# Attention layer of a four-layer graph network: the weighting of the values moves from ScalarE and GpSimd to VectorE

## What is computed

```
q_dst, k_src, v_src = Q[dst], K[src], V[src]
score = sum(q_dst * k_src, axis=-1) / sqrt(16)
attn  = softmax(clip(score, -5, 5), axis=0)     # over all edges, per head
h_out = zeros_like(Q).at[dst].add(attn[..., None] * v_src)
```

## Time and profile before

| | |
|---|---|
| median of 3 runs | 6164.49 us (6153.3 to 6164.83) |
| profiled execution | 6162.2 us, of which the span is 6160.4 us |
| TensorE busy over the span | 5555.2 us (90%) |
| VectorE busy | 4416.3 us (72%) |
| ScalarE busy | 2019.9 us (33%) |
| GpSimd busy | 1360.3 us (22%) |
| the attention's edge stage | from 1076 to 3257 us of the span |
| in it: TensorE / VectorE / ScalarE / GpSimd | 2057.67 / 1666.68 / 868.58 / 724.43 us |

### The profile page before, as it was taken

One profiled execution on the slowest core, in us unless ns is written; L12 is line 12 of the kernel. 1 busy time (PEld: TensorE's weight loads), 2 busy tenths in 40 slices (PEclk: granted clock), 3 DMA queues, 4 the chain that ended last, 5 costly groups with the idle time before them and its releaser, 6 DMA issues. The chain is left out here.

```text
span 6160.4 us, 165256 instructions
## 1 busy us (share of the span) xinstructions
PE 5555.2 (90%) x58225; PEld 4851.5 (79%) x58310; DVE 4416.3 (72%) x7547; ACT 2019.9 (33%) x4615; POOL 1360.3 (22%) x1304
## 2 busy tenths in 40 slices
PE   3999988999999999999996879999999998699986
PEld 2888876888888888888885569999999996456655
DVE  7999942777777777777774457777777774388874
ACT  0000033333433434433432322222222221266651
POOL 1444445333333333333332310000000000200000
PEclk9999999999999999999998989999999997899988
DMA  6444412222222222222220123333333330100000
GB/s 122 149 158 149 158 56 79 88 88 85 85 85 85 88 86 82 88 88 81 88 80 18 37 98 117 121 118 118 115 123 117 119 115 34 57 5 0 0 1 22
DMA packets 206210, 523.66 MB, mean 85 GB/s; under 512 B 33555, under 2 KB 85398, under 8 KB 199318
## 3 DMA queue, kind: packets, MB, share of 16 engines
q1 hardware_dynamic: 195936, 518.35, 24.7%
q10 hardware_dynamic: 10179, 4.02, 0.3%
HBM read 485.12 MB, written 37.19 MB: 85 GB/s over the span
## 5 line engine op out<-in xcount | busy, mean ns | idle before, releaser
L1279 PE MATMUL ps<-kv_table,stage 128*128 128x256 bf16 x7644 | 1252.5, 273 | 29.4 <-DVE stage L1135 27.3
L1251 POOL TENSOR_TENSOR message<-message 128x512 f32<-128x512 f32 (+1 forms) x676 | 724.4, 1072 | 1468.9 <-ACT message L1213 1468.9
L1294 PE MATMUL ps<-message,slot_hot 128*128 128x136 f32 x5200 | 779.2, 292 | 121.2 <-POOL message L1251 102.6
L1667 PE MATMUL ps<-a_table,stage 128*128 128x128 bf16 x7644 | 843.7, 219 | 31.3 <-DVE stage L1550 31.3
L1670 PE MATMUL ps<-window,stage 128*128 128x128 bf16 x7800 | 861.3, 219 | 0.0
L1282 PE MATMUL ps<-window,stage 128*128 128x128 bf16 x7800 | 860.6, 219 | 0.0
L1294 PEld LDWEIGHTS ps<-message,slot_hot 128*128 128x128 f32 x5200 | 649.2, 190 | 212.1 <-POOL message L1251 167.8
L1142 DVE TENSOR_TENSOR slot_hot<-iota,slots 128x512 f32<-128x512 f32 (+1 forms) x676 | 452.5, 669 | 452.7 <-PE ps L1294 452.7
L1569 DVE TENSOR_TENSOR slot_hot<-iota,slots 128x512 f32<-128x512 f32 (+1 forms) x676 | 454.1, 672 | 416.5 <-PE ps L1682 401.4
L1620 ACT ACTIVATE edge<-ps 128x512 f32<-128x512 f32 x624 | 373.4, 598 | 1105.9 <-PE ps L1682 1068.8
L1279 PEld LDWEIGHTS ps<-kv_table,stage 128*128 128x128 bf16 x7644 | 669.1, 98 | 71.5 <-issue 27.9
(11 more groups left out here) (335 smaller groups left out, 7606.3 us busy)
## 6 DMA issues: line engine op xcount, KB each, us to landing
stage<-lists SPq DMA_DIRECT2D x312, 768.0 KB, 4.1
edges<-in_edge_attr SPq DMA_DIRECT2D x52, 1984.0 KB, 7.6
stage<-lists SPq DMA_DIRECT2D x104, 896.0 KB, 5.4
window<-qkv_rows SPq DMA_DIRECT2D x52, 288.0 KB, 4.7
qkv_rows<-kv_table SPq DMA_DIRECT2D x26, 384.0 KB, 2.5
window<-ab_rows SPq DMA_DIRECT2D x52, 192.0 KB, 4.3
qkv_rows<-q_parts SPq DMA_DIRECT2D x26, 192.0 KB, 2.0
ab_rows<-a_table SPq DMA_DIRECT2D x26, 192.0 KB, 2.0
```

What stands on the lines that cost most here:

```text
L1251: pool.tensor_tensor(values, values, message[n % 2][:, 0:nt, D:D + HEADS].unsqueeze(3) .broadcast_to([P, nt, HEADS, HEAD]), ALU.mult).then ...
L1279: nc.tensor.matmul(kv_ps[n % 2][:, i, :], from_src, kv_table[:, tile, q, :], start=(q == 0), stop=(q == 2))
L1294: last = nc.tensor.matmul(ps[:, 6 + d, 0:D + HEADS], slot_hot[n % 2][:, i, :], message[n % 2][:, i, :], start=(tile == 0), stop=(tile == S ...
L1667: nc.tensor.matmul(edge_ps[n % 2][:, i, :], from_src, a_table[:, tile, q, :], start=(q == 0), stop=False)
```

## The change

ScalarE no longer copies V, and GpSimd has no program in this stage. A new VectorE instruction multiplies V, still in PSUM, by the weights and writes `message`. On VectorE `slot_hot` moves from the head of the batch to behind `clipped`, with the new instruction behind it. On ScalarE `exp(n)` now comes ahead of `keep(n+1)`, and it is `exp` that waits for the scatter that frees `message`. A gather waits for `q_kept1` (Q copied) and `message1` (V multiplied) of the batch that used its PSUM buffers.

```diff
                     def batch(pair, g, n):
                         b, s = n % BATCHES, pair * NB2 + n
                         nt = len(batch_tiles(b))
-                        dve.wait_ge(scattered1, s + 1)
-                        dve.tensor_tensor(slot_hot[n % 2][:, 0:nt, :], over_chunks(iota1[:, :], nt),
...
-                        dve.wait_ge(v_kept1, s + 3)
+                        dve.wait_ge(q_kept1, s + 3)
                         dve.wait_ge(score1, s + 1)
...
                         dve.tensor_scalar(clipped[n % 2][:, 0:nt, :], score[:, 0:nt, :], CLIP, -CLIP, ALU.min,
                                           ALU.max).then_inc(clipped1, 1)
+                        dve.wait_ge(scattered1, s + 1)
+                        dve.tensor_tensor(slot_hot[n % 2][:, 0:nt, :], over_chunks(iota1[:, :], nt),
...
+                        dve.wait_ge(weight1, s + 3)
+                        dve.tensor_tensor(message[n % 2][:, 0:nt, 0:D].rearrange("p t (h c) -> p t h c", c=HEAD),
+                                          kv_ps[n % 2][:, 0:nt, D:2 * D].rearrange("p t (h c) -> p t h c", c=HEAD),
+                                          message[n % 2][:, 0:nt, D:D + HEADS].unsqueeze(3)
+                                          .broadcast_to([P, nt, HEADS, HEAD]), ALU.mult).then_inc(message1, 1)
...
                     def keep(pair, n):
...
-                        act.activation(q_kept[n % 2][:, 0:nt, :], q_ps[n % 2][:, 0:nt, :], ACT.Copy)
-                        act.wait_ge(scattered1, s + 1)
-                        act.activation(message[n % 2][:, 0:nt, 0:D], kv_ps[n % 2][:, 0:nt, D:2 * D],
-                                       ACT.Copy).then_inc(v_kept1, 1)
+                        act.activation(q_kept[n % 2][:, 0:nt, :], q_ps[n % 2][:, 0:nt, :], ACT.Copy).then_inc(q_kept1, 1)
 
                     def exp(pair, n):
...
                         act.wait_ge(clipped1, s + 2)
+                        act.wait_ge(scattered1, s + 1)
...
                         for n in range(NB2):
+                            exp(pair, n)
                             if n + 1 < NB2 or ahead:
                                 keep(pair + (n + 1) // NB2, (n + 1) % NB2)
-                            exp(pair, n)
...
-                            pool.tensor_tensor(values, values, message[n % 2][:, 0:nt, D:D + HEADS].unsqueeze(3)
-                                               .broadcast_to([P, nt, HEADS, HEAD]), ALU.mult).then_inc(message1, 1)
...
                     def gather(pair, n):
...
-                        pe.wait_ge(product1, s + 1)
-                        pe.wait_ge(v_kept1, s + 1)
+                        pe.wait_ge(q_kept1, s + 1)
+                        pe.wait_ge(message1, s + 1)
```

More of the change, by code:

```diff
@@ L1069, in gnn_program @@
         gathered1 = sem("gathered1")
-        v_kept1 = sem("v_kept1")
+        q_kept1 = sem("q_kept1")
         product1 = sem("product1")
@@ L1140, in batch @@
                         nt = len(batch_tiles(b))
-                        dve.wait_ge(scattered1, s + 1)
-                        dve.tensor_tensor(slot_hot[n % 2][:, 0:nt, :], over_chunks(iota1[:, :], nt),
-                                          over_columns(slots[:, ds(g, 1), 0, 4 * b:4 * b + nt]
-                                                       .rearrange("p s t -> p (s t)"), P),
-                                          ALU.is_equal).then_inc(slot_hot1, 1)
-                        dve.wait_ge(v_kept1, s + 3)
+                        dve.wait_ge(q_kept1, s + 3)
                         dve.wait_ge(score1, s + 1)
@@ L1158, in batch @@
                                           ALU.max).then_inc(clipped1, 1)
+                        dve.wait_ge(scattered1, s + 1)
+                        dve.tensor_tensor(slot_hot[n % 2][:, 0:nt, :], over_chunks(iota1[:, :], nt),
+                                          over_columns(slots[:, ds(g, 1), 0, 4 * b:4 * b + nt]
+                                                       .rearrange("p s t -> p (s t)"), P),
+                                          ALU.is_equal).then_inc(slot_hot1, 1)
+                        dve.wait_ge(weight1, s + 3)
[3 more added lines that the diff above has]
+                                          .broadcast_to([P, nt, HEADS, HEAD]), ALU.mult).then_inc(message1, 1)
                     def add(j, g, d):
@@ L1195, in _ @@
                     again_total = resorts(act)
-                    act.sem_inc(v_kept1, 2)
                     act.sem_inc(weight1, 2)
@@ L1258, in _ @@
                     pe.sem_inc(gathered1, GATHERED)
+                    pe.sem_inc(message1, 2)
+                    pe.sem_inc(q_kept1, 2)
                     pe.sem_inc(scattered1, 2)
@@ L1288, in scatter @@
                         tiles = batch_tiles(b)
-                        pe.wait_ge(message1, s + 1)
+                        pe.wait_ge(message1, s + 3)
                         pe.wait_ge(slot_hot1, s + 1)
```

## The result

| | before | after |
|---|---|---|
| median, 20 runs each, measured together | 6150.76 us (6144.69 to 6165.96) | 6164.25 us (6159.09 to 6171.15) |
| span of the profiled execution | 6160.4 us | 6158.2 us |
| first to last product of the stage | 2170.8 us | 2176.3 us |
| one group in the middle of the stage | 41.73 us | 41.82 us |

The ratio of the mean times is **1.0018**, with a 95% interval of 1.0011 to 1.0025: the changed kernel is about 11 us slower (7 to 15); the medians themselves are 13.5 us apart. The prediction had said 4 us less. The last line of the table is the mean of 49 groups, the second to the fiftieth of the 52, each from its first product to the next group's.

What follows compares the result with a forecast made beforehand. The loop of scatter, copy of V, exp and GpSimd's multiply was taken to set 41.80 us per group; VectorE's 39.84 plus 1.88 of waits gave 41.72, 4 us less over 52 groups: 6160 us, range 6130 to 6205.

Steps and rivals of the forecast that it cites:

- What bounds the kernel: Attention's edge stage: loop of scatter, copy of V, exp and GpSimd's multiply, 3.23 us per batch; TensorE needs some 3.0.
- The multiply: New VectorE multiply, 676 times: 684 ns, like `product`, between bounds of 597 and 1057; no PSUM surcharge.
- VectorE's chain: Full batch from product to multiply, start to start: 2.77 us; with short batch, masks and add, 39.84 us per group.
- The gather's wait: Loop multiply, gather, copy of Q, product two batches on: 3.64 us; product waits 0.26 us ahead of batches 3, 6, 9.
- The short batch and the wait behind it: Last batch of each group: 1.93 us on VectorE, then the next group's first product waits 1.10 us.
- The sum: Per group, 39.84 us of VectorE plus 1.88 of waits: 41.72 against 41.80, over 52 groups 4 us less.
- The slower one: VectorE's chain some 70 ns per batch longer, between clip and multiply: 37 us, about 6197; chance 0.28.
- The faster one: Clip's gap 0.09 us and loop through TensorE 0.05 us shorter: 20 us less, about 6140; chance 0.25.
- 10 ns per batch on VectorE: Price of added VectorE time: three full batches and the short one absorb it, nine pay, 4.7 us over 52 groups.
- The chances of 0.45, 0.28 and 0.27: No measurable change 0.45; slower 0.28; faster 0.25 plus 0.02 for TensorE becoming the bound, about 5940 us.

Runs made afterwards that it cites:

- run 7: Kernel before, GpSimd's multiply kept: `slot_hot` between reduce and clip, ScalarE copies Q, runs exp, copies V behind the product, which waits only for Q; 5950.86 us, ratio 0.9647.
- run 5: Kernel before, GpSimd's multiply kept: exp(n) ahead of keep(n+1), product waits only for the copy of Q, copy of V waits for product; 6228.27 us, ratio 1.0105.
- runs 3 and 4: Both on the changed kernel: masks of each group's second unit built behind the preceding short batch, 6123.25 us; the clip done twice per batch, 6192.84 us.
- the repeat: Both kernels measured and profiled again, unchanged: before 6164.51 us, ratio 0.9995; changed 6171.89 us, ratio 1.0008.
- run 4: Changed kernel with the same clip run once more into a spare tile on VectorE in each batch; 6192.84 us, ratio 1.0050 to the kernel before.

## Why the prediction was wrong, by its own steps

*What bounds the kernel.* Right, with one thing left out. The loop through the scatter, ScalarE and GpSimd did bound the kernel before: nothing else in it is full, and when the loop is broken without a clash (run 7) the stage falls to TensorE's own 37.55 us per group, against an estimate of 37.5. What I passed over is the reading of the multiplies "of up to 1628 ns" in the earlier trace rows. I used them to explain why the short batch brings nothing and did not ask what makes the same instruction half as long again. It is the clash of run 5 seen from the other side: 97 of the 98 long multiplies overlap a `slot_hot`.

*The multiply.* Right: 684 ns predicted and measured, 676 times. The 65 ns more for a PSUM operand of the Trainium skill's "VectorE: DVE Perf Modes", section on the TRN2 errata, do not show: `slot_hot`, with nothing in PSUM, takes 692 ns.

*VectorE's chain.* Right for the full batch: 2.77 us, each term to within 0.01. The gap from clip to `slot_hot` is 0.12 us and not 0.11 or 0.19. Masks and the add are as priced.

*The gather's wait.* Right for plain batches: a loop of 3.64 us, a wait of 0.27 us (0.26 predicted), ahead of batches 3, 6 and 9. In part that is luck, for two parts of the loop miss in opposite directions: from the multiply's start to the first load it is 0.80 us (0.73 priced), from there to the copy of Q 2.21 (2.27), and then 0.63 to the product (0.64). Counted as the prediction counts, from start to start, all waits are 3 x 0.27 + 1.41 = 2.22 us per group, 115 us in the stage (98 predicted); the profile's 104.6 us are counted from the end of the instruction before, so the two are not to be compared.

*The short batch and the wait behind it: this term failed.* From its product to the next group's first one I had 1.93 + 1.10 = 3.03 us, the loop of 3.64 less 0.61. It is 3.04 us behind the first group of a pair and 3.20 behind the second, 3.12 on average, because the loop there is 3.64 and 3.81 us in turn. That is 0.09 us per group, **5 us**. The batch's own price was wrong as well, without harm to the sum: I took the clip of 399 ns from the earlier trace rows, where it starts inside a GpSimd multiply; it is 175 ns now, the batch costs 1.71 us and not 1.93, and the wait, 1.41 us on average for 1.10, takes up what it saves. In the timeline above the longer loop is 0.80 + 2.29 + 0.72 us: the copy of Q starts 0.08 us later behind the load than elsewhere, the product 0.09 us later behind the copy. In both traces of the changed kernel and those of runs 3 and 4 this is so behind the short batch that ends a pair and not behind the other one, and at a pair's end the written program of each engine goes back to the head of its loop over the pairs. That this turn costs the 0.17 us is likely; no run took it away.

*The sum: the comparison failed too.* I set my 41.72 against 41.80 us per group, which was the whole stage's length divided by its batches and held the longer first group and the longer last but one (44.4 and 43.4 us). The groups in the middle take 41.73. So the forecast was in truth a difference of 0.01 us per group, and the 4 us less was made by comparing a middle group with a mean that included the ends. With the waits as they are, 0.09 and 3 x 0.01 us longer, the sum is 41.84 us, and 41.82 were measured, against 41.73: **4.7 us more**, the sign that was measured. The size fits the traces; of the 7 to 15 us of the first comparison the rest stays open. That the forecast of 6160 us lies near the measured 6164.25 is luck: it started from the profiled execution of the kernel before, 6162.2 us, and the median of that kernel in the comparison is 6150.76.

*The ends.* Not predicted at all: the changed kernel's first group is 2.4 us shorter (42.0 against 44.4) and its last but one 3.9 us longer (47.4 against 43.4), with 4.38 us idle in one place (4.31 in the repeat). That place is the third product of the last pair, which is written out on its own behind the loop over the pairs. The kernel before has such a pause too, in the same group: 2.32 us ahead of a clip (2.09 in the repeat). In all four traces two or three transfers of the kind `instruction`, of 8 KB each on DMA queue 14, start in the pause (at 3182.41, 3182.73 and 3184.59 us in the changed kernel), and in the loop, from 1250 to 3170 us, neither of the two instruction queues has one. So VectorE most likely waits for its program there; I made no run on it.

*The rivals.* The slower one named the clip's gap or the multiply's start, 70 ns per batch; neither happened. The faster one named a loop 0.05 us shorter; it is as long as priced, or longer. That 10 ns per batch on VectorE are 5 us was confirmed by run 4, and it shows the limit of the sum: an equality worked out from twenty terms, with an error of 0.1 us in 41.7, cannot give a sign. The chances of 0.45, 0.28 and 0.27 said so; the point forecast of a gain did not.

## What to carry to other kernels

When a change replaces one loop by another, price the new one against a steady stretch of the old one, group for group, and not against the stage's mean; and do not take an instruction's mean duration if a like one next to it is half as long. An idle stretch in a loop that comes round once a group is free space: work that must be done anyway, moved there, brought 45 us here, by the groups. Before work is taken off GpSimd, ask with which VectorE instruction it overlaps: beside instructions with an operand in PSUM or a reduce it cost next to nothing, while a mask in SBUF that started inside a multiply stood still until its end. Putting the same work in another order brought 218 us where moving it to VectorE brought none.

## What was not expected of the hardware

- An SBUF-to-SBUF instruction on VectorE that starts while a GpSimd multiply runs stands still until its end: the int16 to bf16 mask took 1422 ns for 614, `slot_hot` 1.36 us for 0.69, the half-size one 1070 to 1263 ns for 425, the half-size clip 397 for 175. When VectorE's began first, it kept its time (`slot_hot` 693 ns) and the multiply was the longer one, up to 1628 ns for 1057. A product with an operand in PSUM (684 to 692 ns) and a reduce (686 ns, in the kernel before and in run 7) next to the same multiply were hardly touched.
- VectorE stood 4.3 to 4.4 us, waiting for nothing that the profile's waits show, a few us into the written-out last pair of the changed kernel (2.1 to 2.3 us in the kernel before), with transfers of instructions in the pause.
- The same loop through TensorE and ScalarE took 3.64 and 3.81 us in turn behind the short batch, the longer one where a pair ends.
